# A fused layernorm, attention-like block and feed-forward kernel: another order of work around the first mean coefficient

## The reference, cut to what matters

```python
def _binary_diff_weight(w, base):            # f: W1, W2, W3 with 512 and 1792 features
    d = w - base
    coeff = jnp.mean(jnp.abs(d))
    return base + coeff * jnp.sign(d)
gate = jnp.einsum('bsh,ih->bsi', xn, W1)
up = jnp.einsum('bsh,ih->bsi', xn, W3)
f = jnp.einsum('bsi,hi->bsh', jax.nn.silu(gate) * up, W2)
```

## Time and profile before

| what | value |
|---|---|
| median of 3 runs | 534.44 us |
| the profiled execution | 534.48 us |
| its span (first to last instruction) | 532.7 us |
| TensorE busy | 519.8 us, 98% |
| VectorE, ScalarE, GpSimd busy | 443.0, 328.5, 94.6 us |
| mean products of unit 0 begin | 20.81 us |
| unit 1's gate products begin | 31.36 us |
| `total(UP)` on TensorE | 49.89 us |

### The profile page before, as it was taken

How to read it: one execution, slowest core, us unless ns; L and a number is a source line. 1 busy time by engine, 2 the same in 40 slices (tenths; PEclk the granted TensorE clock), 3 DMA queues, 4 the chain that set the end, 5 groups by cost and what they waited for, 6 DMA issues and landing times.

```text
span 532.7 us, 6530 instructions
## 1 busy us (share of the span) xinstructions
PE 519.8 (98%) x2352; PEld 432.1 (81%) x2352; DVE 443.0 (83%) x520; ACT 328.5 (62%) x455; POOL 94.6 (18%) x106
## 2 busy tenths in 40 slices
PE   4999999999999999999999999999999999999997
PEld 3778888888888888888888888888888888888886
DVE  6989998988896988865898888999999898874447
ACT  2979978557546655446648557968776585464310
POOL 1311002003100310022003121300310040004491
PEclk9999999999999999999999999999999999999999
DMA  8999905045711491059228994941592387127503
GB/s 337 394 401 404 385 8 168 15 137 98 197 54 46 76 234 49 1 106 223 56 70 160 250 217 90 186 101 40 109 187 47 74 163 144 36 46 161 135 20 139
DMA packets 31745, 76.73 MB, mean 144 GB/s; under 512 B 3873, under 2 KB 7297, under 8 KB 31585
## 3 DMA queue, kind: packets, MB, share of 16 engines
q1 hardware_dynamic: 21632, 57.42, 34.4%
q0 software_dynamic: 9792, 18.88, 20.5%
q10 hardware_dynamic: 288, 0.02, 0.0%
HBM read 53.23 MB, written 2.10 MB: 104 GB/s over the span
## 4 chain that ended last, share of the span: by engine, by line
PE 95%; DVE 3%; DMA 1%; issue 0%; ACT 0%; SPq 0%
PE up_ps L1726 28%; PE gate_pair L1726 27%; PE down_pair L1767 11%; PE up_ps L1767 9%; PE down_ps L1767 7%; PE side_ps L1810 2%; PE down_pair L1726 2%; PE down_pair L1677 1%; PE up_ps L1887 1%; PE gate_pair L1887 1%; PE down_pair L1887 1%; DMA xn<-in_x 1%; PE down_pair L1849 1%; PE gate_pair L1767 1%; PE down_pair L1782 1%; DVE xn L1135 1%
## 5 line engine op out<-in xcount | busy, mean ns | idle before, releaser
L1726 PE MATMUL up_ps<-xT,gu 128*128 128x512 f32 x648 | 151.9, 390 | 0.0
L1726 PE MATMUL gate_pair<-xT,gu 128*128 128x512 f32 x624 | 148.4, 390 | 0.9 <-DVE gu L1175 0.9
L1726 PEld LDWEIGHTS up_ps<-xT,gu 128*128 128x128 f32 x648 | 121.6, 188 | 25.1
L1726 PEld LDWEIGHTS gate_pair<-xT,gu 128*128 128x128 f32 x624 | 117.2, 188 | 25.4 <-DVE gu L1175 1.4
L655 POOL DMA_DIRECT2D y<-y_part x64 | 55.4, 878 | 338.3 <-ACT y_part L819 337.1
L806 ACT ACTIVATE h<-up_ps 128x512 fp32r<-128x512 f32 x52 | 31.1, 597 | 110.1 <-DVE up_ps L1242 57.0
L865 ACT ACTIVATE ramp<-codes,bend_bias 128x1536 f32<-128x1536 uint8 x56 | 88.1, 1580 | 1.9 <-DVE acc L1350 1.6
L1350 DVE SCALAR_TENSOR_TENSOR acc<-ramp,acc 128x1536 f32<-128x1536 f32 x42 | 73.6, 1753 | 4.9 <-ACT ramp L865 4.3
L1767 PE MATMUL down_pair<-h,dn 128*128 128x512 f32 x249 | 60.9, 390 | 0.0
L1767 PEld LDWEIGHTS down_pair<-h,dn 128*128 128x128 f32 x249 | 46.8, 188 | 9.8
L1247 DVE TENSOR_TENSOR h<-up_ps,h 128x512 fp32r<-128x512 f32 x52 | 35.8, 688 | 19.7 <-ACT h L806 19.4
(11 more groups left out here) (227 smaller groups left out, 647.2 us busy)
## 6 DMA issues: line engine op xcount, KB each, us to landing
y<-y_part POOLq DMA_DIRECT2D x64, 256.0 KB, 5.1
scale<-in_scales SPq DMA_DIRECT2D x28, 384.0 KB, 5.5
scan_w<-in_w SPq DMA_DIRECT2D x15, 512.0 KB, 11.0
base<-in_mean SPq DMA_DIRECT2D x9, 768.0 KB, 4.4
scan_mean<-in_mean SPq DMA_DIRECT2D x9, 512.0 KB, 10.1
silu_gate<-in_mean SPq DMA_DIRECT2D x6, 512.0 KB, 12.4
codes<-in_codes SPq DMA_DIRECT2D x14, 192.0 KB, 6.0
xn<-in_x SPq DMA_DIRECT2D x4, 512.0 KB, 5.0
```

What stands on the lines that cost most here:

```text
L1726: last = nc.tensor.matmul(ps[:, :], w[:, w_part, hc * P:(hc + 1) * P], xT[:, x_part, hc, th * HALF:(th + 1) * HALF], start=(hc == 0 and w_ ...
```

## The change

- **TensorE**: `early_mean` becomes `early_pass`, one pass at a time: for each half of the tokens first high-high and low(weight)-high, which need no low part of x, then high-low. It begins after the first low part of x (the second half after the second) instead of after four. The thrice-done transposes and the dummy transposes between low parts go; `total(GATE)` moves from inside the last sign products to behind them, with 5 dummy transposes ahead and 8 behind. Unit 1's first product (`project_split`) runs all high-weight passes first, then the low ones.
- **VectorE**: low parts 0 and 1 of x come before `scan_subtract(1)`, and 2 to 7 directly behind it. Unit 1 is made in three pieces of 128, 128 and 256 columns, each scaled by the total straight from PSUM, and its low part is one instruction. The factor 1 / (1792 x 512) goes into the matrix of ones.
- **GpSimd**: unit 0's low part waits for the last normalised tile instead of `scan_subtract(1)`. Units 0, 1 and 2 are subtracted in a row behind `scan_subtract(1)`.
- **ScalarE**: unit 0's high part comes before the signs of scan tile 0; the signs of scan tile 2 move behind unit 1's pieces, `unit_sum(1)` before `sum_apart(2)`, `unit_high(3)` before the signs of tile 5.

```diff
@@ -26,6 +26,7 @@
+PIECES = [(0, P), (P, 2 * P), (2 * P, HID)]
@@ -36,8 +37,7 @@
-AGAIN = 3
-WARM_LOW = {1: 6, 2: 5, 3: 5}
+WARM_TOTAL = [5, 8]
@@ -617,7 +616,7 @@
         def _(pool):
...
-            nc.gpsimd.memset(ones[:], 1.0).then_inc(const_ready, 1)
+            nc.gpsimd.memset(ones[:], 1.0 / (INTER * HID)).then_inc(const_ready, 1)
@@ -643,7 +642,7 @@
             def early_low():
...
-                pool.wait_ge(scan_diff, dve_tiles(1))
+                pool.wait_ge(xn_ready, TT)
@@ -658,10 +657,9 @@
             pool.wait_ge(scan_mean_loaded[0], 16)
             nc.gpsimd.tensor_copy(next_gate, mean_tile(0)[:, 0:HID]).then_inc(next_kept, 1)
             early_low()
+            pool.wait_ge(scan_diff, dve_tiles(1))
             unit_subtract(0)
-            pool.wait_ge(xT_lo, 4)
             unit_subtract(1)
-            pool.wait_ge(scan_diff, dve_tiles(2))
             unit_subtract(2)
             unit_subtract(4)
             pool.wait_ge(gu_lo, FIRST)
@@ -738,14 +736,14 @@
             def unit_signs(u):
...
-            def split_high(half):
-                sl = slice(half * HID // 2, (half + 1) * HID // 2)
-                if half == 0:
-                    act.wait_ge(half_made, 1)
+            def split_high(n):
+                sl = slice(*PIECES[n])
+                if n < 2:
+                    act.wait_ge(piece_made, n + 1)
...
-                                     ).then_inc(half_hi if half == 0 else gu_hi, 1)
+                                     ).then_inc(piece_hi if n < 2 else gu_hi, 1)
...
             def unit_high(u):
@@ -977,8 +975,8 @@
             nc.scalar.activation(stats[:, 0, 0:BENDS], bend_bias[:, :], ACT.Silu)
             x_high(2)
             x_high(3)
+            early_high()
             scan_signs(0)
-            early_high()
             x_high(4)
             x_high(5)
             x_high(6)
@@ -986,16 +984,16 @@
             scan_signs(1)
             unit_sum(0)
             early_sign()
+            unit_sum(1)
             sum_apart(2)
-            unit_sum(1)
-            scan_signs(2)
             sum_apart(3)
             unit_sum(2)
             unit_sum(3)
             unit_signs(1)
             unit_signs(2)
-            split_high(0)
-            split_high(1)
+            for n in range(len(PIECES)):
+                split_high(n)
+            scan_signs(2)
             scan_signs(3)
             unit_high(2)
             unit_signs(3)
@@ -1003,8 +1001,8 @@
             silu(0, 1)
             scan_signs(4)
             silu(1, 0)
+            unit_high(3)
             scan_signs(5)
-            unit_high(3)
             next_gate_high()
             unit_sum(4)
             silu(1, 1)
@@ -1147,10 +1145,12 @@
+            def keep_coeff(m):
+                dve.wait_ge(total_ready, m + 1)
+                nc.vector.tensor_copy(coeff[:, m:m + 1], side_ps[:, m:m + 1]).then_inc(coeff_ready, 1)
             def take_coeff(m):
-                dve.wait_ge(total_ready, m + 1)
-                nc.vector.tensor_scalar(coeff[:, m:m + 1], side_ps[:, m:m + 1], 1.0 / (INTER * HID), None, ALU.mult
-                                        ).then_inc(coeff_ready, 1)
+                keep_coeff(m)
...
             def unit_make(u):
@@ -1159,22 +1159,13 @@
-            def split_make(half):
-                sl = slice(half * HID // 2, (half + 1) * HID // 2)
+            def split_make(n):
+                sl = slice(*PIECES[n])
...
+                dve.wait_ge(total_ready, GATE + 1)
...
-                                               coeff[:, GATE:GATE + 1], unit_base(SPLIT_UNIT)[:, sl], ALU.mult, ALU.add
-                                               ).then_inc(half_made if half == 0 else unit_made, 1)
-            def split_low(half):
-                sl = slice(half * HID // 2, (half + 1) * HID // 2)
-                if half == 0:
-                    dve.wait_ge(half_hi, 1)
-                else:
-                    dve.wait_ge(gu_hi, SPLIT_UNIT + 1)
-                nc.vector.tensor_tensor(unit_split(SPLIT_UNIT)[:, LO, sl], unit_base(SPLIT_UNIT)[:, sl],
-                                        unit_split(SPLIT_UNIT)[:, HI, sl].bitcast(f32), ALU.subtract
-                                        ).then_inc(half_lo if half == 0 else gu_lo, 1)
+                                               side_ps[:, GATE:GATE + 1], unit_base(SPLIT_UNIT)[:, sl], ALU.mult, ALU.add
+                                               ).then_inc(piece_made if n < 2 else unit_made, 1)
...
             def unit_low(u):
@@ -1521,24 +1512,22 @@
             scan_subtract(0)
             for t in range(4, TT):
                 normalise(t)
+            x_low(0)
+            x_low(1)
             scan_subtract(1)
-            for t in range(4):
+            for t in range(2, TT):
                 x_low(t)
-            x_low(4)
-            x_low(5)
             scan_subtract(2)
-            x_low(6)
-            x_low(7)
             scan_subtract(3)
             scan_subtract(4)
             unit_subtract(3)
             scan_sum(4)
             take_part(GATE)
-            take_coeff(GATE)
-            split_make(0)
-            split_make(1)
-            split_low(0)
-            split_low(1)
+            for n in range(len(PIECES)):
+                split_make(n)
+            keep_coeff(GATE)
+            unit_low(SPLIT_UNIT)
+            dve.wait_ge(coeff_ready, 1)
             early_scale(0)
             unit_make(2)
             early_add(0)
@@ -1658,32 +1647,30 @@
-                for _ in range(AGAIN if t == TT - 1 else 1):
-                    for c in range(HC):
-                        last = nc.tensor.matmul(x_ps[t][:, c * P:(c + 1) * P], xn[:, t, c * P:(c + 1) * P], ident[:],
-                                                is_transpose=True, start=(c == 0), stop=(c == HC - 1))
+                for c in range(HC):
+                    last = nc.tensor.matmul(x_ps[t][:, c * P:(c + 1) * P], xn[:, t, c * P:(c + 1) * P], ident[:],
+                                            is_transpose=True, start=(c == 0), stop=(c == HC - 1))
...
-            for low, count in WARM_LOW.items():
-                pe.wait_ge(xT_lo, low)
-                warm(early_ps[0], count)
-            def early_mean(th):
-                pe.wait_ge(gu_lo, 1)
-                pe.wait_ge(xT_lo, TT // 2 * (th + 1))
+            def early_pass(th, w_part, x_part):
+                if w_part == LO:
+                    pe.wait_ge(gu_lo, 1)
+                elif x_part == LO:
+                    pe.wait_ge(xT_lo, TT // 2 * (th + 1))
+                else:
+                    pe.wait_ge(gu_hi, 1)
+                    pe.wait_ge(xT_lo, th + 1)
+                    pe.wait_ge(xT_hi, TT // 2 * (th + 1))
                 for hc in range(HC):
-                    for w_part, x_part in PASSES:
-                        nc.tensor.matmul(early_ps[th][:, :], gu_weight(0, GATE)[:, w_part, hc * P:(hc + 1) * P],
-                                         xT[:, x_part, hc, th * HALF:(th + 1) * HALF],
-                                         start=(hc == 0 and w_part == x_part == HI),
-                                         stop=(hc == HC - 1 and w_part == LO))
+                    nc.tensor.matmul(early_ps[th][:, :], gu_weight(0, GATE)[:, w_part, hc * P:(hc + 1) * P],
+                                     xT[:, x_part, hc, th * HALF:(th + 1) * HALF],
+                                     start=(hc == 0 and w_part == x_part == HI), stop=(hc == HC - 1 and x_part == LO))
...
             def early_signs(th):
...
                 for hc in range(HC):
-                    if th == 1 and hc == 2:
-                        total(GATE)
                     for x_part in (HI, LO):
@@ -1696,9 +1683,7 @@
             def project(k, kind, th, total_within=None):
-                if k == SPLIT_UNIT and kind == GATE and th == 0:
-                    pe.wait_ge(half_lo, 1)
-                elif kind == GATE or k <= FIRST:
+                if kind == GATE or k <= FIRST:
@@ -1720,8 +1705,6 @@
                 for hc in range(HC):
-                    if hc == HC // 2 and k == SPLIT_UNIT and kind == GATE and th == 0:
-                        pe.wait_ge(gu_lo, gu_count(k, kind))
                     for w_part, x_part in PASSES:
@@ -1730,6 +1713,22 @@
+            def project_split():
+                w = gu_weight(SPLIT_UNIT, GATE)
+                for hc in range(HC):
+                    if hc < 2:
+                        pe.wait_ge(piece_hi, hc + 1)
+                    if hc == HC // 2:
+                        pe.wait_ge(gu_hi, SPLIT_UNIT + 1)
+                    for x_part in (HI, LO):
+                        nc.tensor.matmul(gate_bank(SPLIT_UNIT, 0)[:, :], w[:, HI, hc * P:(hc + 1) * P],
+                                         xT[:, x_part, hc, 0:HALF], start=(hc == 0 and x_part == HI), stop=False)
+                pe.wait_ge(gu_lo, gu_count(SPLIT_UNIT, GATE))
+                for hc in range(HC):
```

(22 more changed lines are left out.)

## The result

The changed kernel takes 535.54 us (median of 20 runs, 535.39 to 535.72), the kernel before 534.46 in runs on the same chip. The ratio is 1.0018 with a 95% interval of 1.0012 to 1.0025: slower by 1.0 us, while the two medians differ by 1.08. That is less than the 0.2% that the forecast set as the bound of "no change", with the interval reaching across it. The spans of the two profiled executions are 533.8 and 532.7 us. The forecast was 535.2.

The account below looks back on a forecast made before the run. TensorE was taken as the bound (95% of the chain): 0.5 us early at unit 1, but 0.80 late at the second sum. 534.48 + 0.80 = 535.28, 535.2 against the median; own range 534.8 to 535.7, wider range 533.6 to 536.0.

Parts of the forecast that it names:

- The front: Mean products and low parts of x: TensorE starts at about 17.8 instead of 20.81, which gives nothing by itself.
- When T comes: VectorE's work up to take_part(GATE): scan_subtract(2) loses 1.0 us to GpSimd, so T is 29.45, later by 0.68.
- T: The moment VectorE starts the first partial sum, take_part(GATE): 28.77 before the change, forecast at 29.45.
- The small collision before it: On VectorE, scan_subtract(1) at 18.25 meets GpSimd making unit 0's low part and ends at 19.64: 0.25 us.
- From T to unit 1: From the partial sum to unit 1's first matmul: 1.41 instead of 2.59 us, start at 30.86, TensorE 0.5 us early.
- From unit 1 to the second sum: GpSimd's unit 4 holds unit_low(2), delaying silu(0, 1) and then ScalarE's last absolute sum by 1.27; total(UP) at 50.69, 0.80 late.
- The third signs later, at no cost: Third signs done at about 31.5 instead of 24.99, VectorE's slot reloaded some 6 us later: taken as 0.
- To the end: Behind the second sum TensorE has no wait to the end, so the 0.80 us stay.
- its rival: Unit 2's low part still goes before GpSimd's unit 4; unit_high(3), waiting for unit_make(3), then counts: 534.5 us, chance 0.15.
- No first collision: T = 28.77, unit 1 at 30.18, 1.18 us early, of which only 0.36 stay: 534.1 us, chance 0.15.
- The clock falls: TensorE's idling at the first sum drops it to 1.2 GHz, costing 2.65 us, 1.30 free: 536.6 us, chance 0.07.

Follow-up runs that it names:

- the first experiment: Changed kernel with low parts 6 and 7 of x back behind the third difference and GpSimd's old wait before unit 2: 534.87 us.
- the experiment on the pieces alone: Kernel before with unit 1 in three PSUM-scaled pieces, later third signs, earlier unit_high(3), first sum behind sign products: 535.82 us; with the sum back among them: 534.79 us.
- the second experiment: Changed kernel with only one wait put back, so GpSimd subtracts unit 2 only after VectorE's third difference: 535.53 us.
- the last kernel: The first experiment's kernel with unit_high(3) back behind the signs of tile 5 and total(UP) between the halves of chunk 4: 534.07 us.

## Why the prediction was right, point by point

- **The front** began at 17.75 (17.8 forecast) and gave nothing by itself. That its transposes cost nothing was not tested apart; the old front with them and the new one without them (534.79 and 534.87 us) are alike. Right.
- **When T comes**: 29.32 against 29.45. The subtraction at 23.08 took 2.13 us (2.2 forecast). Shown by the first experiment: without that meeting T is 28.72. The small collision before it was called 0.25 us; the forecast's own times give 0.17, and the subtraction at 18.16 took 1.41 us, 0.19 more than 1.22. The sum had used its times.
- **From T to unit 1**: 30.79, forecast 30.86. TensorE was 0.57 early, 0.5 forecast. But the three pieces take longer on VectorE. The first starts at T + 0.72, not T + 0.64. The profile puts its wait to ScalarE's sign, but unit 1's sign, the first of the two behind 28.87, is done by about 29.5. What it waits for is the sum: it starts 0.50 to 0.51 us behind the start of a sum that had been waited for, in the changed kernel and in eight others, whichever engine is named, and 0.40 behind one that was not waited for (the two kernels of the experiment on the pieces alone). The second starts 0.15 us after it could, a pause for which the profile names no cause and that I had put at 0. `early_scale(0)` is at T + 3.08, not T + 2.75.
- **From unit 1 to the second sum**: `unit_low(2)` at 34.98 taking 1.35 us (34.78 and 1.6), `silu(0, 1)` at 36.97 (37.05), `unit_sum(4)` at 41.92 (42.00), `total(UP)` at 50.67 (50.69), idle 1.08 (1.3). The times were right. The reason given was too narrow: it named the silu behind the collision as the one path, and delaying GpSimd changed nothing. `unit_make(3)` and `unit_high(3)` are a second path of nearly the same length. The forecast had this path only in its rival. There was some luck too: VectorE was 0.2 us later at `unit_low(2)` than forecast, and this did not show, because GpSimd's end at 35.78 sets when that low part is done.
- **The third signs later, at no cost.** The stream of loads does have a hole. In the view by stretches, 33 to 36 us have a DMA share of 0.92 and 300 GB/s, against 1.03 and 399 before. No instruction of VectorE or ScalarE waits for a load behind it, and the kernel with the signs early and the clock held has no hole and is not faster, so the hole cost nothing that can be seen. What the edit gives is T, 0.5 to 0.9 us earlier in the two profiles with early signs, which the forecast did not see and which is worth next to nothing.
- **To the end.** +0.80 forecast, 1.08 measured. The difference is the sum after a wait (0.11) and the 0.15 us that appear after 306 us, which is left open. The term that was too small is the one that let the 0.80 us stay to the end unchanged.
- **The rivals.** "No first collision" (534.1) is the first experiment: 534.87. So even that case would have been slower than the rival said. 0.82 us of wait stayed at the second sum, which stood at 49.81 where the rival had 49.53; the longer sum and the extra after 306 us take 0.25 more. It moved the last absolute sum by nothing, while it is 0.3 us late. "The clock falls" did not happen, but three other kernels showed it: with this waiting time it is near. Where the profiles show 1.7 us of idling ahead of the sum it falls in some runs, and where they show 3.3 us in all.

## What to carry to other kernels

An earlier start of the bound engine is worth only what the next shared result allows: before moving work forward, write down the spare time at each later wait (here 0.4 us at the second sum) and count the gain against it. GpSimd's arithmetic wants to lie beside VectorE's PSUM work, and a reordering that removes that cover makes each of its instructions a stop for VectorE. When TensorE must wait a microsecond or more, check the granted clock behind the wait; a few transposes without use cost nothing there. Where it does not wait, they stand in the way (0.55 us for five, with the pieces alone).

## What the runs showed of the hardware

- A VectorE subtraction with two SBUF inputs and a GpSimd subtraction exclude each other both ways. Started second, VectorE's 1024 columns end 1.08 to 1.09 us behind GpSimd's end (four cases: 22.20, 36.02, 24.13 here, 26.74 in the second experiment), its 512 columns 0.55 us behind. Started second, GpSimd takes 2.21 to 2.22 instead of 1.29 us (two cases). The Trainium skill (SBUF — State Buffer, SBUF: two separate sides) calls this an exclusive lock that whichever starts first holds for its whole instruction. The trace agrees: no progress, not half speed.
- After waits the clock fell to the 1.2 GHz level: with 1.71 us of idling in the profile, five of eight runs have a mean clock of 0.997; with 1.72 us and 0.88 more behind the sum, seven of eleven have 0.996 or 0.997; with 3.33 us, all five have 0.993 to 0.997. Idle times of 1.26 and 1.08 us left it at 2.4 GHz. Transposes in the wait held it in both kernels where they were added.
- A column sum (two matmuls of one column) adds 0.24 to 0.25 us behind a wait and 0.14 without one (0.19 at 29.05 in the kernel before). It adds 0.25 also at 49.89 in the last kernel, where no wait is listed, though the twelve matmuls from 46.98 would be through at 49.70.
